# Selective scan of a fused perceiver kernel: logarithms, late gates and delta's parts in another order

## What is computed

```python
deltaA = jnp.exp(jnp.einsum('bld,dn->bldn', delta, a))
deltaBu = jnp.einsum('bld,bln,bld->bldn', delta, b, u)
def step(h, inp):
    dA_t, dBu_t, c_t = inp
    h = dA_t * h + dBu_t
    y = jnp.einsum('bdn,bn->bd', h, c_t)
    return (h, y)
```

## Time and profile before

| | us |
|---|---|
| median of 3 runs | 678.44 |
| the profiled execution's own time | 678.84 |
| its span | 677.1 |
| VectorE busy (share of span) | 471.5 (70%) |
| ScalarE busy | 367.8 (54%) |
| GpSimd busy | 229.6 (34%) |
| TensorE busy | 606.3 (90%) |

### The profile page before, as it was taken

The page is one execution under the profiler, slowest core; times in us unless marked ns, Lnnn a source line. Parts: engine busy times, 40 slices in busy tenths (PEclk is TensorE's granted clock), DMA queues, the critical chain, the costliest instruction groups (busy, mean ns, idle before and its releaser), DMA issues. The chain is left out here.

```text
span 677.1 us, 11619 instructions
## 1 busy us (share of the span) xinstructions
PE 606.3 (90%) x4390; PEld 459.3 (68%) x4390; DVE 471.5 (70%) x793; ACT 367.8 (54%) x692; POOL 229.6 (34%) x182
## 2 busy tenths in 40 slices
PE   4999998899995677878878999999999999999997
PEld 4455544454354666767767888887787767889897
DVE  3733333346856999999999546678978768876554
ACT  1411111125768799999999543433566456556342
POOL 2000000000029799999989300033652020231000
PEclk9999999999997799999999999999999979999999
DMA  8999999994902122233331000000100022110000
GB/s 314 398 395 394 389 389 390 395 324 138 269 6 94 62 95 94 94 109 110 105 106 40 1 1 1 16 1 18 35 3 2 1 63 78 51 60 1 32 1 31
DMA packets 31294, 86.47 MB, mean 128 GB/s; under 512 B 8076, under 2 KB 19816, under 8 KB 29064
## 3 DMA queue, kind: packets, MB, share of 16 engines
q1 hardware_dynamic: 31096, 85.67, 35.3%
q10 hardware_dynamic: 144, 0.06, 0.1%
HBM read 83.50 MB, written 1.11 MB: 125 GB/s over the span
## 5 line engine op out<-in xcount | busy, mean ns | idle before, releaser
L764 POOL TENSOR_TENSOR dbu<-du,bs 128x1024 f32<-128x1024 f32 x63 | 149.2, 2396 | 11.6 <-DVE w_in L1010 8.2
L889 ACT ACTIVATE weighed<-T,CT 128x256 f32<-128x256 f32 x222 | 94.1, 575 | 8.2 <-PE T L1089 7.8
L1010 DVE TENSOR_TENSOR_SCAN w_in<-hS,dbu 128x1024 f32<-128x1024 f32 x42 | 94.7, 2273 | 2.2 <-POOL dbu L764 1.7
L878 ACT ACTIVATE hS<-delta,negA 128x504 f32<-128x504 f32 x128 | 89.6, 795 | 6.1 <-DVE w_in L1010 2.8
L1089 PE MATMUL T<-ident,w_in 128*128 128x128 f32 x336 | 47.3, 284 | 23.4 <-ACT weighed L889 13.5
L1103 PE MATMUL Y<-ident,weighed 128*128 128x128 f32 x512 | 67.7, 275 | 0.1
L1089 PEld LDWEIGHTS T<-ident,w_in 128*128 128x128 f32 x336 | 37.3, 143 | 34.1 <-DVE w_in L1010 28.7
L1103 PEld LDWEIGHTS Y<-ident,weighed 128*128 128x128 f32 x512 | 58.7, 142 | 0.8 <-DVE sres L1031 0.3
L297 PE MATMUL O<-cN,pT 128*64 128x256 f32 x384 | 46.7, 385 | 6.7 <-DMA cN<-in_ctx 6.7
L1010 DVE TENSOR_TENSOR_SCAN xn<-hS,dbu 128x1024 f32<-128x1024 f32 x22 | 50.0, 2274 | 3.4 <-ACT hS L878 3.3
L383 POOL COPY w_xp<-w_xp 128x64 f32<-128x64 f32 x3 | 0.6, 236 | 146.7 <-DMA w_out<-in_w_out 146.7
(11 more groups left out here) (424 smaller groups left out, 1365.7 us busy)
## 6 DMA issues: line engine op xcount, KB each, us to landing
cT<-in_ctxT SPq DMA_DIRECT2D x8, 3202.0 KB, 22.5
cN<-in_ctx SPq DMA_DIRECT2D x8, 3072.0 KB, 25.2
bs<-b_rows SPq DMA_DIRECT2D x32, 512.0 KB, 3.6
raw_w<-in_w SPq DMA_DIRECT2D x16, 256.0 KB, 2.9
w<-in_w SPq DMA_DIRECT2D x7, 256.0 KB, 8.1
vs<-vx SPq DMA_DIRECT2D x8, 136.0 KB, 2.4
x<-in_x SPq DMA_DIRECT2D x2, 512.0 KB, 5.5
cR<-in_ctx SPq DMA_DIRECT2D x8, 128.0 KB
```

The lines of the kernel that those rows point to most:

```text
L764: e.tensor_tensor(dbu[s % NB][:, :, :], half(m.du, s // DS), row, ALU.mult).then_inc(s_bu, 1)
L878: i = e.activation(by_batch(A[s % 2][:, j * HALF:(j + 1) * HALF]), by_batch(m.delta[:, c, h * HALF:(h + 1) * HALF]), ACT.Exp, scale=m.negA ...
L889: i = e.activation(weighed[s % 2][:, q * Q:(q + 1) * Q], T[:, q * Q:(q + 1) * Q], ACT.Copy, scale=c_of(s, q))
L1010: e.tensor_tensor_scan(S[s % NS], A[s % 2][:, :], dbu[s % NB][:, :, :].rearrange("p c n -> p (c n)"), 0.0, ALU.mult, ALU.add).then_inc(s_h, 1)
```

## The change

- ScalarE runs exp and ln of the first half's two groups, then the second half's |v|, exp and ln, all ahead of `decays(0)`. Before, ln of groups 1 and 2 stood between decays(1) and decays(2).
- The second half's gates (blocks 12 to 15) are left raw by VectorE (`raw_gate`, all four instead of two) and get their SiLU from ScalarE at steps 62 and 63 (`last_gates`). The third unit's gating therefore becomes a copy of Y into `gated`, and GpSimd multiplies it by the gate at the end.
- The second half's positive part stays in PSUM (tiles `dq`), and VectorE's `add_parts` reads it from there, ahead of the scan. The first half's `add_parts` (four), its first two `steps_by_input` and `dbu[0]` are all GpSimd's.
- TensorE runs all projections before the folding's transposes; the copies qT and kTb move from VectorE to ScalarE.

```diff
-            for n in range(4, 8):
-                absolute(n)
-            gate_part(4)
-            gate_part(5)
             e.preload_act_table_set("natural_log_exp_and_others")
...
-            exponential(0)
-            logarithm(0)
+            for g in range(2):
+                exponential(g)
+                logarithm(g)
+            for n in range(4, 8):
+                absolute(n)
+            exponential(2)
+            logarithm(2)
...
-            decays(0)
+            e.wait_ge(s_fp, pe_at["wT", 0])
+            e.activation(qT, Y[:, 0:HALF], ACT.Copy).then_inc(s_wt, 1)
+            e.wait_ge(s_fp, pe_at["wT", 1])
+            e.activation(kTb[:, :, 0:D], Y[:, HALF:2 * HALF]...).then_inc(s_wt, 1)
...
+            def last_gates(c0):
+                for c in (c0, c0 + 1):
+                    e.wait_ge(s_rg, c + 1)
+                    g = m.sres[:, c, HALF:2 * HALF]
+                    e.activation(g, g, ACT.Silu).then_inc(s_ge, 1)
...
+                if s == STEPS - 2:
+                    e.preload_act_table_set("silu_and_others")
                 for b in (1, 0) if on_dve(s) else (0, 1):
                     weigh(s, b)
+                if s == STEPS - 2:
+                    last_gates(0)
+            last_gates(2)
...
+                dst = dq[n % 4] if n >= CH else m.du[:, n, 0:HALF]
+                e.tensor_scalar(dst, dq[n % 4], col(k, "dtb", n % CH), 0.0, ALU.add, ALU.max)
...
+                e.tensor_tensor(m.delta[:, c, hs], dq[c], m.delta[:, c, hs], ALU.add).then_inc(s_dl, 1)
...
+            for c in (0, 2, 1):
+                add_parts(c)
+            e.wait_ge(s_dl, 2)
+            zeros(0)
+            add_parts(3)
+            e.wait_ge(s_dl, 4)
+            zeros(1)
...
+                if u == 2:
+                    e.tensor_copy(k.gated[:, j, :], Y[:, j * HALF:(j + 1) * HALF]).then_inc(s_yg, 1)
+                    return
...
-                if s in (2, 3):
-                    for c in (2 * s - 4, 2 * s - 3):
-                        add_parts(1, c)
```

More of the change, by code:

```diff
@@ L649, in mamba @@
         s_dl = sem("m_dl")
-        s_du = sem("m_du")
         s_dup = sem("m_dup")
@@ L656, in mamba @@
         s_ge = sem("m_ge")
-        s_b0 = sem("m_b0")
+        s_sg = sem("m_sg")
         s_ct = sem("m_ct")
@@ L674, in mamba @@
         block = ctx.enter_context(nc.Block())
-        pe_steps = ([("in", n) for n in range(2, 8)] + [("xj", 0), ("in", 8), ("dt", 0), ("in", 9), ("in", 10), ("xj", 1),
-                    ("wT", 0), ("wT", 1), ("in", 11), ("dt", 1), ("in", 12), ("in", 13), ("in", 14), ("in", 15), ("CT", 0),
+        pe_steps = ([("in", n) for n in range(2, 8)] + [("xj", 0), ("in", 8), ("dt", 0), ("in", 9), ("in", 10), ("in", 11),
+                    ("xj", 1), ("in", 12), ("dt", 1), ("in", 13), ("in", 14), ("in", 15), ("wT", 0), ("wT", 1), ("CT", 0),
                     ("vo", 0), ("bv", 0), ("A", 0), ("b", 0), ("vo", 1)])
@@ L681, in mamba @@
                     ("row", 0), ("u", 5), ("gate", 0), ("u", 6), ("abs", 0), ("abs", 1), ("abs", 2), ("abs", 3), ("u", 7),
-                    ("gate", 1), ("gate", 2), ("gate", 3), ("abs", 4), ("abs", 5), ("abs", 6), ("abs", 7), ("gate", 4),
-                    ("gate", 5), ("exp", 3), ("neg", 0), ("exp", 0), ("ln", 0), ("exp", 1), ("exp", 2), ("ln", 1), ("ln", 2)]
+                    ("gate", 1), ("gate", 2), ("gate", 3), ("exp", 3), ("neg", 0), ("exp", 0), ("ln", 0), ("exp", 1), ("ln", 1),
+                    ("abs", 4), ("abs", 5), ("abs", 6), ("abs", 7), ("exp", 2), ("ln", 2)]
         pe_at = {step: i + 1 for i, step in enumerate(pe_steps)}
@@ L737, in steps_by_input @@
                 if h:
-                    e.wait_ge(s_dl, c + 2)
+                    e.wait_ge(s_dl, CH)
                 else:
-                    e.wait_ge(s_dup, (None, 1, 3, 5)[c])
+                    e.wait_ge(s_dup, (1, 2, 5, 6)[c])
                 hs = slice(h * HALF, (h + 1) * HALF)
                 e.tensor_tensor(m.du[:, c, hs], m.delta[:, c, hs], m.u[:, c, hs], ALU.mult).then_inc(s_dup, 1)
-            for s in range(1, STEPS):
+            for c in range(2):
+                add_parts(c)
+            for c in range(2):
+                steps_by_input(0, c)
+            for s in range(STEPS):
                 if s == 1:
[L746 to L749, removed]
+                    add_parts(2)
+                    add_parts(3)
                 if s in (6, 10):
@@ L767, in _ @@
                             rowvec(k, "outb").unsqueeze(1).to_broadcast([P, TILES, D]), ALU.add).then_inc(s_xo, 1)
+            for c in range(2):
+                e.wait_ge(s_yg, 4 + c + 1)
+                e.wait_ge(s_ge, c + 1)
+                e.tensor_tensor(k.gated[:, c, :], k.gated[:, c, :], m.sres[:, c, HALF:2 * HALF], ALU.mult).then_inc(s_sg, 1)
         @block.scalar
@@ L867, in decays @@
                 if s == 0:
-                    e.wait_ge(s_dl, 1)
-                    e.wait_ge(s_dup, 1)
+                    e.wait_ge(s_dup, 2)
                 if s == DS:
-                    e.wait_ge(s_dup, 5)
+                    e.wait_ge(s_dup, 6)
                 if s in (2 * DS, 3 * DS):
-                    e.wait_ge(s_dl, 2 * (s // DS) - 1)
+                    e.wait_ge(s_dl, CH)
                 if s >= 2:
@@ L891, in weigh @@
                 i.then_inc((s_e0, s_e1)[b], 1)
-            decays(0)
+            e.wait_ge(s_fp, pe_at["wT", 0])
+            e.activation(qT, Y[:, 0:HALF], ACT.Copy).then_inc(s_wt, 1)
+            e.wait_ge(s_fp, pe_at["wT", 1])
+            e.activation(kTb[:, :, 0:D], Y[:, HALF:2 * HALF].rearrange("p (c n) -> p c n", c=KD), ACT.Copy).then_inc(s_wt, 1)
             e.wait_ge(s_fp, pe_at["vo", 0])
             e.activation(vT, T[:, HALF:2 * HALF], ACT.Copy).then_inc(s_vo, 1)
-            exponential(1)
-            exponential(2)
+            decays(0)
             decays(1)
-            logarithm(1)
-            logarithm(2)
             decays(2)
@@ L948, in positive, with add_parts, raw_gate @@
                 e.wait_ge(s_fa, ac_at["abs", n])
[L949 to L957, removed]
+                dst = dq[n % 4] if n >= CH else m.du[:, n, 0:HALF]
+                e.tensor_scalar(dst, dq[n % 4], col(k, "dtb", n % CH), 0.0, ALU.add, ALU.max).then_inc(s_rz, 1)
+            def add_parts(c):
+                e.wait_ge(s_fa, ac_at["ln", 2])
+                e.wait_ge(s_rz, 2 * CH)
+                hs = slice(HALF, 2 * HALF)
+                e.tensor_tensor(m.delta[:, c, hs], dq[c], m.delta[:, c, hs], ALU.add).then_inc(s_dl, 1)
+            def raw_gate(n):
+                e.wait_ge(s_fp, pe_at["in", 8 + n])
+                e.tensor_scalar(m.sres[:, n % CH, HALF:2 * HALF], zp[n % 4], col(k, "inb", CH + n % CH), None, ALU.add
+                                ).then_inc(s_rg, 1)
             for n in range(2 * CH):
@@ L966, in _ @@
             keep_rows()
+            raw_gate(4)
+            for n in range(CH, 2 * CH):
+                positive(n)
+            raw_gate(5)
+            raw_gate(6)
+            raw_gate(7)
             e.wait_ge(s_fa, ac_at["u", 2 * CH - 1])
             for c in range(KD):
[L969 to L981, removed]
-            zeros = lambda r: e.memset(A[r].rearrange("p (b l) -> p b l", l=L)[:, :, 0], 0.0).then_inc(s_z, 1)
[L984 to L992, removed]
+                i = e.tensor_copy(kTb[:, c, D:D + 1], col(k, "bk5", c))
+            i.then_inc(s_wt, 1)
+            zeros = lambda r: e.memset(A[r].rearrange("p (b l) -> p b l", l=L)[:, :, 0], 0.0).then_inc(s_z, 1)
+            for c in (0, 2, 1):
+                add_parts(c)
+            e.wait_ge(s_dl, 2)
+            zeros(0)
+            add_parts(3)
+            e.wait_ge(s_dl, 4)
+            zeros(1)
             e.wait_ge(s_fp, pe_at["bv", 0])
@@ L995, in _ @@
             e.tensor_copy(CT[:, :, :], T[:, 0:TILES * 2 * DS].rearrange("p (t n) -> p t n", n=2 * DS)).then_inc(s_ct, 1)
[L996 to L1000, removed]
             def scan(s):
                 e.wait_ge(s_A, s + 1)
[L1004 to L1007, removed]
+                e.wait_ge(s_bu, s + 1)
                 if s >= NS:
@@ L1155, in _ @@
             project(10)
+            project(11)
             x_proj(1)
+            project(12)
+            dt_proj(1)
+            project(13)
+            project(14)
+            project(15)
             e.wait_ge(k.s_w5, k.n_w5)
             for w in range(2):
-                e.wait_ge(s_fa, ac_at["gate", w])
+                e.wait_ge(s_rg, w + 1)
                 for c in range(KD):
@@ L1164, in _ @@
                 i.then_inc(s_fp, 1)
[L1165 to L1171, removed]
+            e.wait_ge(s_rg, 3)
             for t in range(TILES):
@@ L1175, in _ @@
             e.wait_ge(k.s_rows, 16)
-            e.wait_ge(s_rg, 2)
+            e.wait_ge(s_rg, 4)
             for c in range(KD):
@@ L1185, in _ @@
             i.then_inc(s_fp, 1)
-            e.wait_ge(s_wt, 2)
-            e.wait_ge(s_fa, ac_at["gate", 5])
```

(1 more changed line is left out.)

12 lines of the change are left out of this document (3 added, 9 removed).

## The result

The changed kernel takes 666.56 us, the median of 4 runs (665.63 to 668.02), against 678.39 (677.01 to 678.97, 4 runs); the ratio is 0.983, 95% interval 0.980 to 0.985. Run again beside one of the experiments it took 667.77 (ratio 0.984, 0.981 to 0.987). The prediction was 667.5 us, with a range of 664 to 672.

The account below looks back on a forecast made before the run. The prediction took ScalarE and VectorE together to hold the loop, with time to be had at its start. From 678.84 us it took 11.7 for the start and added 0.4 for the end: 667.5 us, range 664 to 672.

Parts of the forecast that it names:

- 11.7 forecast: Loop's start: scan 7 comes 11.7 us earlier, the middle of counts by ScalarE (11.4) and VectorE (11.9).
- the gating row: VectorE's gating at 260.71, one operand in PSUM beside busy GpSimd: 0.64 us, taken as the price of each PSUM addition.
- 0.4 named: Loop's end: the moved table load and SiLUs cost 0.4 us.
- my bounds: Loop's end: bounds on the price of the moved table load and SiLUs, 0 to 1.6 us.
- "held" addition: VectorE adding two SBUF tensors beside GpSimd: 1.7 us each, 3.41 the pair.
- The wait ahead of gate 3: ScalarE's idle of 5.44 us for block 11, before the loop, was to fall near 0.
- ScalarE sets the pace: Loop's start: a decays and a weighing, 2.6 us, outlast a scan of 2.2, so ScalarE runs without gaps.
- The front is held: Rival, ahead of the loop: PSUM adds or positive parts take 1.7 us, decays(0) 3 to 5 late; 671.5 us, chance 0.14.
- a rival of its own: Rival, loop's start: TensorE's clock falls all the same, 2.5 us plus 0.6 come back; 670.5 us, chance 0.09.

Follow-up runs that it names:

- gates_ahead: Changed kernel with gates 4 and 5 given back to ScalarE as SiLUs ahead of the table load, none of it in the loop: 676.77 us, ratio to before 0.997.
- block11_late: Changed kernel with block 11 projected behind x_proj(1) again: 674.28 us, ratio to before 0.994.
- idle_tensore: Changed kernel with two useless ScalarE copies of 128x2048 between decays(2) and the folding copies, so TensorE idles: 672.44 us, ratio to before 0.992.
- positives_in_sbuf: Changed kernel with the second half's positive parts written to SBUF instead of PSUM, additions still ahead of the scan: 673.92 us, ratio to before 0.992.
- block 11 alone: Kernel before with only block 11's projection moved ahead of x_proj(1): 678.36 us, ratio to before 1.000.
- adds_in_loop: Changed kernel with the second half's positive parts in SBUF and its four additions back in the loop (steps 2 and 3): 671.59 us, ratio to before 0.991.

## Why the prediction was right

The mechanism and the size both came out, and no two large errors had to cancel. From the block's first instruction, scan 0 comes 2.5 us earlier than before the change, the first weighing 6.0 and scan 7 12.1, for 11.7 forecast; the end of the block takes 0.6 of it back, and the loop from scan 7 to scan 63 gives 0.4, about what two traces of one kernel differ by. That makes the 11.9 of the block. Half of the 0.9 us between 667.5 and 666.56 is the base: I had started from an execution of 678.84, where the median is 678.39.

The places hold when the 0.8 us of the earlier start is taken off. The last logarithm was set at 197.6 and ends at 196.87 (196.8 wanted). GpSimd's first dbu ends at 196.13 (196.2). The PSUM additions cost 0.64 each, as the gating row said, and the four positive parts written back to PSUM 2.73 in all, 0.68 each: no hold, as assumed for want of a row. Scan 0 is at 200.22 (200.4), the first weighing at 206.11 (206.2), scan 7 at 220.13 (220.3). From scan 7 to scan 63 it takes 142.29 us, 142.67 before and 142.63 in the changed kernel's second trace: nothing, as counted. The end costs 0.3 us up to TensorE's last product (12.38 us behind scan 63's start for 12.08), for 0.4 named; another 0.3 lies in the wait at the block's barrier (0.79 against 0.51), which I had not counted. It is there in every trace in which GpSimd multiplies the third unit's gates at the end, also with the table load moved behind the loop (0.79), and not in that of gates_ahead, where GpSimd does not (0.48). Why is open.

The drain that the Trainium skill (ScalarE: Activation LUTs, section What ACT_TABLE_LOAD costs) adds to a table load isn't there: 1.30 us from the load's start to the weighing behind it, and the load starts 0.02 us behind the weighing ahead of it. One slip of the prediction hangs on it: by the page the end would have cost 1.8 us, and I wrote that this is within my bounds, which end at 1.6.

Three statements were wrong without harm to the sum. A "held" addition takes 1.7 us only as the mean of 0.66 and 2.85, so a front that is held costs more than I priced. The wait ahead of gate 3 is 1.03 us, not near 0. And "ScalarE sets the pace" in the steady loop isn't shown: taking work from it gave nothing. In the loop's start ScalarE is idle for 0.9 us of 29.5. What holds the steady pair at 4.97 us stays open.

The prices of the rivals were too low. "The front is held" was priced at 3 to 5 us late and 671.5 us; in the run it was 5.3, and 8.0 with the clock's part, and the kernel took 673.92. Each of the four runs that delayed ScalarE or VectorE by 3.5 to 8 us ahead of the loop or in it also lost 1.1 to 5.1 us to TensorE's clock and what hung on it: 3.5 became 4.7 (block11_late), 3.9 became 5.9 (idle_tensore), 5.3 became 8.0 (positives_in_sbuf) and 8.1 became 13.2 (gates_ahead). I had treated the clock as a rival of its own, where it came with each of these delays.

The parts don't add up: undoing one costs 6.4 (additions), 4.7 (block 11) or 12.6 (late gates) of an in-block gain of 11.9 (by the medians 5.0, 7.7 and 10.2 of 11.8), and block 11 alone brings 0.4 in its trace and nothing in the timing. They are links of one chain: the early block frees ScalarE, the late gates let it go on to the table load, and the exponentials fill the time. No run puts the logarithms alone back between the decays. The nearest evidence is adds_in_loop, which leaves them ahead of the scan: its first weighing comes 6.2 us earlier than before the change, as in the changed kernel, and what it loses is lost behind that. So about half of the gain is made before the first weighing and goes with the logarithms' new place and what makes room for it; how it divides among these is not shown.

## What to carry to other kernels

Where a loop's start runs well below its steady pace (here 4.2 us a step against 2.5), list what stands between its first steps and ask what could run in an earlier wait of the same engine. Moving the block that ended that wait brought nothing until work was there to fill it. Where VectorE must add beside a busy GpSimd, leave one operand in PSUM: 0.7 us against up to 2.8. A mean over a pair can hide such a hold, so read the instructions one by one. Price each stall of a few us on the way to TensorE with the stall and the clock behind it.

## What the runs showed of the hardware

In idle_tensore the granted clock stood at 0.50 (1.2 of 2.4 GHz) from 208 to 212 us, where TensorE had idled 5.1 us before its first turn, and eight transposes then took 1.94 us instead of 1.06; after 1.25 us of idling, in the changed kernel, it was 1.00. A fall to 0.57 (block11_late, the mean of 4 us) or 0.50 (gates_ahead) in the middle of folding stretched a product from 2.00 to 3.57 or 3.80 us, on the path. A delay of 3.5 us cost 4.7 so, and one of 8.1 cost 13.2.

A VectorE addition of two SBUF tensors (128x512) took 0.66 or 0.67 us (the kernel before) when it started ahead of GpSimd's product and 2.8 when it started during one of 128x1024; it then ended 0.55 us behind the product, which itself took up to 2.82 us (adds_in_loop) instead of 2.37. With one operand in PSUM the addition took 0.68 beside GpSimd's additions and 0.72 beside such a product.
